# Layer 4: statistics of the second normalisation as row totals on ScalarE, and the maxima's rounded operands a slot earlier

## The reference, cut to what matters

```python
def _layernorm(x, eps=1e-05):
    m = jnp.mean(x, axis=-1, keepdims=True)
    v = jnp.var(x, axis=-1, keepdims=True)
    return (x - m) / jnp.sqrt(v + eps)

x = _layernorm(x + _L0_attn_ref(x, ...))            # layer 0, causal
x = _layernorm(x + _L0_xattn_ref(x, ctx, ...))      # layer 1
x = _layernorm(x + _L0_ffn_ref(x, ...))             # layer 2: causal attention and four experts
x = _layernorm(x + _L1_attn_ref(x, ...))            # layer 3
x = _layernorm(x + _L1_xattn_ref(x, ctx, ctx, group_prob, mask, ...))   # layer 4
x = _layernorm(x + _L1_ffn_ref(x, ...))             # eight routed experts, top 1, with a capacity
```

## Time and profile before

| | |
|---|---|
| runs | 1475.51 us median of 3 (1475.17 to 1483.09) |
| profiled execution | 1476.44 us, of which the span 1474.7 us |
| TensorE busy | 1357.1 us, 92% |
| VectorE busy | 1025.0 us, 70% |
| ScalarE busy | 861.4 us, 58% |
| GpSimd busy | 549.1 us, 37% |
| granted clock of TensorE | 0.97 of full speed over the span |

### The profile page before, as it was taken

One profiled execution on the slowest core, in us unless ns is written; L12 is line 12 of the kernel. 1 busy time (PEld: TensorE's weight loads), 2 busy tenths in 40 slices (PEclk: granted clock), 3 DMA queues, 4 the chain that ended last, 5 costly groups with the idle time before them and its releaser, 6 DMA issues. The chain is left out here.

```text
span 1474.7 us, 41105 instructions
## 1 busy us (share of the span) xinstructions
PE 1357.1 (92%) x16926; PEld 957.6 (65%) x16926; DVE 1025.0 (70%) x2589; ACT 861.4 (58%) x1402; POOL 549.1 (37%) x727
## 2 busy tenths in 40 slices
PE   8999999999979999999999999988998877758997
PEld 5677656666656767667776676755655444438997
DVE  4577777767685556466563544686899999847896
ACT  1355666667556555464654646454557776636774
POOL 4146775623331121232222211341333443542766
PEclk8799999999999999999999999989999999878999
DMA  8589777755360312301011010143877544115451
GB/s 166 89 149 181 148 157 139 125 110 73 60 82 3 44 27 35 46 10 45 17 31 46 2 52 3 46 110 80 136 180 126 97 82 67 39 56 192 146 190 56
DMA packets 100297, 126.90 MB, mean 86 GB/s; under 512 B 7900, under 2 KB 90099, under 8 KB 97552
## 3 DMA queue, kind: packets, MB, share of 16 engines
q1 hardware_dynamic: 96496, 118.84, 39.8%
q0 software_dynamic: 2032, 4.24, 0.9%
q10 hardware_dynamic: 1584, 1.20, 0.3%
HBM read 51.10 MB, written 9.51 MB: 41 GB/s over the span
## 5 line engine op out<-in xcount | busy, mean ns | idle before, releaser
L972 ACT ACTIVATE probs<-eslot 128x1024 f32<-128x1024 f32 x188 | 192.6, 1025 | 105.6 <-PE eslot L703 104.4
L1534 POOL TENSOR_SCALAR_AFFINE_SELECT probs<-probs 128x512 f32<-128x512 f32 x128 | 82.5, 646 | 332.5 <-ACT probs L970 332.2
L674 PE MATMUL mslot<-stack 48*128 48x256 f32 (+2 forms) x1110 | 166.7, 337 | 37.8 <-DVE mx L1202 26.5
L674 PEld LDWEIGHTS mslot<-stack 48*128 48x128 f32 (+1 forms) x1110 | 99.7, 190 | 127.0 <-issue 61.7
L1191 DVE TENSOR_REDUCE mx_blocks<-mslot 128x3 f32<-128x384 f32 x214 | 114.7, 554 | 56.6 <-PE mslot L674 40.2
L1473 POOL TENSOR_SCALAR ave<-amv 128x2 f32<-128x2 f32 x64 | 23.6, 368 | 308.5 <-DVE amv L1109 267.0
L970 ACT ACTIVATE probs<-eslot 128x512 f32<-128x512 f32 (+1 forms) x256 | 111.7, 490 | 44.4 <-PE eslot L703 43.8
L703 PE MATMUL eslot<-stack 50*128 50x256 f32 (+1 forms) x1264 | 126.2, 276 | 6.5 <-ACT probs L972 3.5
L718 PE MATMUL bank<-probs,v 128*32 128x256 f32 (+1 forms) x2048 | 125.8, 364 | 2.2 <-POOL probs L1534 1.1
L1208 DVE TENSOR_REDUCE mx<-mslot 128x4 f32<-128x1024 f32 x64 | 78.1, 1221 | 69.9 <-PE mslot L674 69.3
L518 PE MATMUL bank<-slot_rows_sb,l 128*32 128x256 f32 x2048 | 113.8, 380 | 0.0
(11 more groups left out here) (279 smaller groups left out, 3409.0 us busy)
## 6 DMA issues: line engine op xcount, KB each, us to landing
stack<-split SPq DMA_DIRECT2D x192, 256.0 KB
w<-in_w SPq DMA_DIRECT2D x16, 1024.0 KB
stack<-split SPq DMA_DIRECT2D x96, 128.0 KB
slot_rows_sb<-in_proj SPq DMA_DIRECT2D x15, 256.0 KB, 4.7
slot_rows<-hTf SPq DMA_DIRECT2D x4, 650.0 KB, 4.8
slot_rows_sb<-slot_rows SPq DMA_DIRECT2D x4, 650.0 KB, 5.5
expert_rows<-slot_rows SPq DMA_DIRECT2D x8, 260.0 KB, 2.7
hT<-in_xT SPq DMA_DIRECT2D x8, 256.0 KB, 7.8
```

The lines of the kernel that those rows point to most:

```text
L674: mm = pe.matmul(ps[:, first:first + m], queries(u, h, k)[:, qt * P:(qt + 1) * P], keys(u, h, k)[:, 0:m], start=clear, stop=clear or qt == ...
L972: e = act.activation(PR[:, k, :, :, :].rearrange("p a k q -> p (a k q)"), ps[:, :, :, :].rearrange("p a k q -> p (a k q)"), ACT.Exp, scale ...
L1534: pool.affine_select(diagonal, diagonal, [[0, 2 * TT], [1, P]], ALU.is_ge, 0.0, base=0, channel_multiplier=-1)\
```

## The change

"even" moves from 30 to 31, its statistics go to ScalarE as four ACTIVATEs with row totals (mean, and mean of squares), and GpSimd works out the variance from them; "even rows" moves from 31 to 32; "parts" gets rank 5.5 in slot 7 instead of rank 0 in the next slot. LAST_PLACE keeps its 30 and 30. TMP takes the elementwise results, which nobody reads.

```diff
-         "w end": 26, "norm": 30, "even": 30, "xT": 30, "even rows": 31, "logits": 32, "chances": 32, "rank": 33,
+         "w end": 26, "norm": 30, "even": 31, "xT": 30, "even rows": 32, "logits": 32, "chances": 32, "rank": 33,
...
-        put(at(8), ENDS, "parts", u, 0)
+        put(at(7), WEIGHT - 0.5, "parts", u, 0)
...
 (ScalarE)
+            elif step == "even":
+                act.wait_ge(*evened(u))
+                if u > 4 * B:
+                    act.wait_ge(*pool_step.at("even", u - 1))
+                else:
+                    act.wait_ge(*dve_step.at("split", u - 1))
+                for tt in range(TT):
+                    act.activation(TMP[:, 0, tt, :], X[u % B][:, tt, :], ACT.Identity, scale=1.0 / C,
+                                   accum_out=MV[CTX][:, tt, 0:1])
+                    a = act.activation(TMP[:, 1, tt, :], X[u % B][:, tt, :], ACT.Square, scale=C ** -0.5,
+                                       accum_out=MV[CTX][:, tt, 1:2])
+                a.then_inc(*act_step("moments", u))
 (VectorE)
-            elif step == "even":
-                dve.wait_ge(*evened(u))
-                if u > 4 * B:
-                    dve.wait_ge(*pool_step.at("even", u - 1))
-                statistics(CTX, X[b], ("even", u), False)
 (GpSimd, step "even")
-                inverse_roots(CTX, ("even", u), eps_n)
-                pool.wait_ge(*pool_step.at("rstd", "even", u))
+                pool.wait_ge(*act_step.at("moments", u))
+                then(pool.tensor_tensor(VE[CTX][:, 1, :], MV[CTX][:, :, 0], MV[CTX][:, :, 0], ALU.mult))
+                then(pool.tensor_tensor(VE[CTX][:, 0, :], MV[CTX][:, :, 1], VE[CTX][:, 1, :], ALU.subtract))
+                then(pool.tensor_scalar(VE[CTX][:, 0, :], VE[CTX][:, 0, :], eps_n, None, ALU.add))
+                then(pool.tensor_tensor(RSTD[CTX][:, 0, :], VE[CTX][:, 0, :], powers[:, 0, :], ALU.pow))
                 then(pool.tensor_tensor(VE[CTX][:, 1, :], MV[CTX][:, :, 0], RSTD[CTX][:, 0, :], ALU.mult))
```

## The result

The changed kernel takes 1489.75 us (median of 7 runs, 1484.91 to 1497.24), the kernel before 1475.74 us on the same chip (7 runs, 1475.17 to 1486.49). The ratio is 1.0085, 95% interval 1.0063 to 1.0106: 9 to 16 us slower. The forecast of 1481.3 us had the sign and less than half of the size.

What follows compares the result with a forecast made beforehand. It held TensorE behind ScalarE and GpSimd's path, not VectorE alone, to bound layer 4's slots, ScalarE the last unit. Terms 0 + 0 + 2.5 + 1.3 + 2.0 = +5.8 us gave 1481.3 us, range 1468 to 1490.

Steps and rivals of the forecast that it cites:

- the rival that GpSimd takes the port first: Four units of layer 4: GpSimd's weighting of pair 4 precedes VectorE's of pair 5; +8 on top, 1489 us; chance 0.15.
- Parts: 0: Parts step moved from slot 0 to slot 7: VectorE's order in layer 4 unchanged, layer 2 covered; worth 0.
- The statistics leave VectorE: 0: VectorE in layer 4: 0.95 us less per unit, but TensorE's scores hold slot 7; taken as 0, bounds 0 and -7.6 us.
- Totals 1.8 us, the gate's products 0.7 late: ScalarE, slot 7: four ACTIVATEs with totals take 1.8 us; TensorE's gate products start at 1213.1 instead of 1212.38.
- GpSimd's chain 2.8 us, weighting done 9.35 to 9.95 us behind slot 7: GpSimd, slot 7: six small operations take 2.8 us ahead of pair 4's weighting, which ends at 1217.7 or 1218.3.
- Slot 1 0.3 us late: VectorE's slot 1 starts at about 1216.4 against 1216.10, spending the rounding's 1.25 us gain with 0.3 us on top.
- Pair 6's exponential +2.0: ScalarE: even rows wait for GpSimd's chain, so pair 6's exponential comes at 1218.6 instead of 1216.60; covered.
- For the four units I count 0.0: Four layer 4 units, slot 7 ending 1149.6 to 1240.7 us: cover used up, cost 0.0, each with bounds -0.9 and +2.0.
- +3.8 for the last unit and the slot 7 after it: Past 1269 us, no cover left: two terms, +2.5 for the last unit and +1.3 for the slot 7 after it.
- The last unit, +2.5: ScalarE as bound past 1269 us: statistics, rows ahead of pair 6 and waiting for GpSimd; +2.0 to +2.8, taken +2.5.
- The slot 7 after it, +1.3: Pair 4's weighting behind GpSimd's chain makes pair 6's exponential 3 us later, pair 7's takes 1.7 back; +1.3.
- Tail +2.0: Tail: unit 38's statistics and rows delay ScalarE, +1.5; two more small GpSimd operations for unit 39, +0.5; sum +2.0.

Runs made afterwards that it cites:

- e1: The kernel before with only the parts step moved to slot 7 ahead of its weighting; 1475.46 us, ratio 0.9972.
- e6: The kernel of e3 with the even rows one slot later, behind pair 6's exponential, totals still on ScalarE; 1480.19 us, ratio 1.0023.
- e4: The changed kernel without the four ACTIVATEs that make the totals, GpSimd's chain waiting for x alone; 1480.36 us, ratio 1.0024.
- e9: The kernel of e6 plus an empty wait of VectorE for GpSimd's normalised x where its statistics stood; 1478.95 us, ratio 1.0007.
- after: The changed kernel itself, with the whole change, against the kernel before; 1489.75 us, ratio 1.0085.
- e10: The changed kernel plus only an empty wait of VectorE for GpSimd's normalised x where its statistics stood; 1490.27 us, ratio 1.0076.
- e2: The changed kernel with the parts step put back to the start of slot 0; 1491.56 us, ratio 1.0075.
- e5: The kernel before with only the even rows one slot later (slot 0 instead of 7), statistics still on VectorE; 1476.44 us, ratio 1.0001.
- e3: The changed kernel with GpSimd's chain as its own step behind the weighting of pair 4 instead of ahead; 1487.0 us, ratio 1.0040.

## Why the prediction was right in sign and short in size

By its own steps. Measured against the profiled executions the sum was 5.8 us and is 15.85; by the ratio it is some 12.5 us. That 1489.75 us lies in my range of 1468 to 1490 is luck in part: the upper end came from the rival that GpSimd takes the port first, which didn't come, and my forecast's own range ended at 1486.

- *Parts: 0.* Right, shown by e1; and e6 shows that the unblocked rounding buys no later slot.
- *The statistics leave VectorE: 0.* Right for VectorE's busy time but for 0.9 us once (e4). Wrong for what else the instruction did: its wait kept VectorE off GpSimd's normalisation in unit 37. I had counted "up to 0.9 us" of relief there. The profiles show a loss of 2.6 us (e6 to e9) to 3.4 us (after to e10), 0.97 of it the collision.
- *Totals 1.8 us, the gate's products 0.7 late.* Measured 1.59 us; the gate's products begin 4.65 us behind slot 7 instead of 4.03, +0.6, their wait 1.34 us. The Trainium skill, "ScalarE: Activation LUTs", section "What ACT_TABLE_LOAD costs", has a formula that gives an estimate of 399 ns for one such ACTIVATE; the trace agrees, 401. The overlap of 93 ns that it states doesn't show: one follows the other after 0.40 us, with the read of the total, 0.19 us, for which it has no price, beside them.
- *GpSimd's chain 2.8 us, weighting done 9.35 to 9.95 us behind slot 7.* Measured 2.2 us, and 9.62. The rival that GpSimd takes the port first didn't come: VectorE's weighting led by 0.17 us and it was GpSimd's that took 3.27 us.
- *Slot 1 0.3 us late.* In this unit it was not late at all (7.75 in both); behind slot 7 of unit 35 it was (9.39 against 6.89, and 7.76 in e2). *Pair 6's exponential +2.0.* Measured +1.45.
- *"For the four units I count 0.0".* By the marks 34 to 38 they cost 4.5 us, but 2.7 of that is the mark, which moved from 5.13 to 7.81 us behind slot 7 at unit 38 and not at unit 34. From slot 7 of unit 34 to that of unit 39 it is 3.3 us in the changed kernel at a clock of 0.92, and 0.0 in e2 with the same order there, at 0.97 as before. e10, which differs ahead of slot 7 of unit 39 only by the empty wait, has 3.4 at 0.92. So 0.0 was right in one of three executions, and the 3.3 or 3.4 us of the others came with the slower clock, for which I had no term. The account beneath it had a gap, too: I asked whether VectorE's weighting of pair 6 is reached in time. What is reached late is TensorE's `w`, queued behind ScalarE's read of `o`, which the totals and the rows delay along with pair 6 (8.67 us behind slot 7 with the rows alone in e5, 8.25 before, 9.70 in the changed kernel); slot 2 is 1.05 us late, and the slots behind it take that back, in full in one unit and to 0.57 us in another.
- **The step that fell short: +3.8 for the last unit and the slot 7 after it.** From slot 7 of unit 39 to `w`'s read of unit 38 it is +10.7 (by the marks, 38 to that read, +9.4). Both terms were too small, for different reasons.
- *The last unit, +2.5.* Measured +4.0, to 0.02 us the same in after, e2, e3 and e10 (15.51 to 15.53 against 11.53). The rows alone cost 0.2 there (e5), the totals with the rows behind pair 6 2.05 (e6), both ahead of it 4.0 (e3), of which 0.63 is the rows' wait for GpSimd's chain. The slack ahead of TensorE's `w` is spent once.
- *The slot 7 after it, +1.3.* Measured +6.7, and 5.1 in e2. I had no term for the port: 3.6 go when the wait is put back (after to e10), 2.7 from e6 to e9, and in e9 nothing is left of the loss (21.83 against 22.03). In e10 3.1 are left. How they divide between GpSimd's chain ahead of its weighting and the rows' slot is open: the order on GpSimd makes 2.7 from after to e3, and 1.05 from e2 to e3.
- *Tail +2.0.* Measured +1.9; 0.5 of it is the two more small operations for the last unit, as written (9.72 us in e6 against 9.19 from VectorE's work on its gate's logits to the second program).

Where the 15.85 us went, in the order in which edits took them back in the profiles: chain ahead of the weighting 4.3 (after to e3), rows ahead of pair 6 6.1 (e3 to e6), the unguarded port 2.5 (e6 to e9), and 3.05 that remain with the totals (e9 against before). The granted clock follows: 0.88, 0.90, 0.91, 0.92, 0.94. No single one of these steps is shown by the times: the ratios are 1.0085, 1.0040, 1.0023 and 1.0007, and the intervals of neighbours overlap. Clear of each other are the changed kernel (from 1.0063) and e6 (to 1.0037) or e9 (to 1.0028). And the first step is smaller than the 4.9 us between e2 and the changed kernel. How much of each step is the clock's and how much the wait's own I didn't separate.

## What to carry to other kernels

An instruction that looks like mere work can be a guard: before moving it, read what it waits for, what stands behind it in its queue, and which engine shares a port with that. Slack is no sum of shares: in the last unit two moves that cost 0.2 and 2.05 us alone cost 4.0 together, since they delay the same queue. Put the marks of a comparison where the change doesn't move them, and profile the same order twice before a few us are given a cause. When an engine gets new work ahead of a read that TensorE waits for, follow TensorE's queue first, not the engine relieved.

## What the chip showed that I had not expected

- A wait of TensorE can cost more than itself: sixteen 128x32 by 128x256 products took 1.87 us behind a wait of 1.43 us and 1.07 us behind one of 0.40; four turns 1.09 us behind 3.55 and 0.66 behind 2.60. It isn't a rule of the wait's length: in e3 and the changed kernel the turns behind 3.55 us took 0.66. Nor of the order: at the same place of the changed kernel and of e2 the same wait was followed by either speed.

```profile
1254.20 1.93 PE L518 MATMUL bank<-weight_w,yT 128*32 128x256 f32 x16 [1.40 <-ACT mT L1044]
```
```profile
1252.96 1.07 PE L518 MATMUL bank<-weight_w,yT 128*32 128x256 f32 x16 [1.41 <-ACT mT L1044]
```

- Over the stretch from unit 34's mark, TensorE is busy 12.4 us longer in the changed kernel and 6.1 us longer in e2, with the same 2316 instructions.
- ScalarE's row total of a 128x256 ACTIVATE comes for about 0.1 us: 401 ns, one every 0.40 us, the accumulator's read of 0.19 us beside it. The 0.1 us is an estimate: at the overlap of 0.10 us that the pair of rows has, ACTIVATEs of 401 ns would follow each other after 0.30.
- An empty wait on VectorE brought 2.6 us in the profile of one kernel and 3.4 in that of another. The times of neither show it.
- Whether VectorE's weighting and GpSimd's normalisation hold each other up depended on which started first: weighting first, GpSimd's second instruction took 2.18 us instead of 1.22; normalisation first, both took 1.22.
